# Second products two sequences behind the first, two sets of transposed rows, layer norm moved to the head of VectorE's list

## The reference

```python
h = gelu(einsum('bsh,bhi->bsi', x, Wi[expert]) + bi[expert])     # 512 -> 2048
o = einsum('bsi,bih->bsh', h, Wo[expert]) + bo[expert]           # 2048 -> 512
r = o + x
y = (r - mean(r)) * rsqrt(var(r) + 1e-12) * gamma[expert] + beta[expert]
x0, x1, x2, x3 = features of y by fours
out = stack([x0*ct + x1*st, -x0*st + x1*ct, x2*cp + x3*sp, -x2*sp + x3*cp])
```

## Time and profile before

| | |
|---|---|
| time of 3 runs, median (lowest to highest) | 2797.54 us (2796.03 to 2798.73) |
| profiled execution, its own time | 2791.9 us |
| its span, first to last instruction | 2790.2 us |
| TensorE, matmuls busy | 2679.8 us, 96% |
| VectorE busy | 1959.2 us, 70% |
| GpSimd busy | 1368.4 us, 49% |
| ScalarE busy | 930.0 us, 33% |
| granted TensorE clock, mean | 0.991 of full speed |

### The profile page before, as it was taken

How to read it: one execution, slowest core, us unless ns; L and a number is a source line. 1 busy time by engine, 2 the same in 40 slices (tenths; PEclk the granted TensorE clock), 3 DMA queues, 4 the chain that set the end, 5 groups by cost and what they waited for, 6 DMA issues and landing times.

```text
span 2790.2 us, 54938 instructions
## 1 busy us (share of the span) xinstructions
PE 2679.8 (96%) x12306; PEld 1208.7 (43%) x12307; DVE 1959.2 (70%) x4919; ACT 930.0 (33%) x1689; POOL 1368.4 (49%) x1619
## 2 busy tenths in 40 slices
PE   2899999999999999999999999999999999999998
PEld 1344444444444444444444444444444444444443
DVE  4577677677777777777777777777766776777676
ACT  4333333333333333333333333333333333333332
POOL 4778717872017872577600577607872677500000
PEclk9899999999999999999999999999999999999999
DMA  4577556865446865658644658646776667444343
GB/s 159 143 135 191 128 134 152 182 150 118 85 94 158 179 147 129 147 126 193 151 84 93 148 126 194 149 83 166 169 150 120 166 126 175 113 92 89 83 98 65
DMA packets 742569, 376.01 MB, mean 135 GB/s; under 512 B 682816, under 2 KB 682944, under 8 KB 733824
## 3 DMA queue, kind: packets, MB, share of 16 engines
q1 hardware_dynamic: 677568, 173.95, 36.6%
q0 software_dynamic: 25984, 130.29, 14.7%
q10 hardware_dynamic: 38976, 71.32, 8.1%
HBM read 174.13 MB, written 33.55 MB: 74 GB/s over the span
## 4 chain that ended last, share of the span: by engine, by line
PE 79%; DMA 6%; DVE 5%; issue 4%; POOL 2%; DVEq 2%; ACT 1%; ACTq 0%; SPq 0%; POOLq 0%
PE o_ps L850 40%; PE z_ps L834 39%; DMA hT<-h 2%; DMA xT<-x 2%; DMA xbuf<-in_x 2%; DVE z_ps L647 1%; DVEq L196 1%; ACT z_ps L472 1%; DVE h L657 0%; ACT x L467 0%; DVE ln L674 0%; DVE y L702 0%; DVE r_ps L673 0%; ACTq L196 0%; POOL wo L340 0%
## 5 line engine op out<-in xcount | busy, mean ns | idle before, releaser
L850 PE MATMUL o_ps<-wo,hT 128*128 x6144 | 1419.7, 381 | 24.0 <-DMA hT<-h 15.7
L834 PE MATMUL z_ps<-wi,xT 128*128 x6096 | 1401.7, 380 | 31.0 <-DMA xT<-x 18.8
L850 PEld LDWEIGHTS o_ps<-wo,hT 128*128 128x128 f16 x6144 | 603.6, 98 | 758.2 <-issue 41.7
L834 PEld LDWEIGHTS z_ps<-wi,xT 128*128 128x128 f16 x6096 | 597.0, 98 | 759.6 <-issue 56.8
L472 ACT ACTIVATE z_ps<-z_ps 128x512 f32<-128x512 f32 x512 | 299.1, 584 | 1760.6 <-DVE z_ps L647 1746.2
L647 DVE SCALAR_TENSOR_TENSOR z_ps<-z_ps,tok,bi_all 128x512 f32<-128x512 f32 x512 | 387.4, 757 | 217.4 <-PE z_ps L834 156.8
L406 POOL TENSOR_TENSOR wi<-staged 128x512 f32<-128x512 f32 x112 | 117.7, 1051 | 646.6 <-DVE r_ps L667 635.5
L657 DVE SCALAR_TENSOR_TENSOR h<-z_ps,tok,h 128x512 f16<-128x512 f32 x512 | 380.2, 743 | 7.4 <-ACT h L478 6.9
L478 ACT ACTIVATE h<-z_ps,tok 128x512 f16<-128x512 f32 x512 | 351.8, 687 | 19.0
L652 DVE SCALAR_TENSOR_TENSOR x<-xbuf,tok,x 128x512 f16<-128x512 f16 (+1 forms) x128 | 121.1, 946 | 189.2 <-ACT x L467 189.2
L702 DVE SCALAR_TENSOR_TENSOR y<-r_ps,rot,y 128x128 f32<-128x128 f32 x512 | 195.2, 456 | 5.0 <-ACT y L485 2.0
(11 more groups left out here) (126 smaller groups left out, 1408.8 us busy)
## 6 DMA issues: line engine op xcount, KB each, us to landing
staged<-in_L_cond_Wi POOLq DMA_DIRECT2D x56, 1024.0 KB, 6.0
staged<-in_L_cond_Wo POOLq DMA_DIRECT2D x56, 1024.0 KB, 6.8
xbuf<-in_x ACTq DMA_DIRECT2D x128, 256.0 KB, 3.6
out<-y ACTq DMA_DIRECT2D x128, 256.0 KB, 3.5
hT<-h SPq DMA_TRANSPOSE x512, 4.2
bi_all<-in_L_cond_bi POOLq DMA_DIRECT2D x7, 1024.0 KB, 9.7
wi<-in_L_cond_Wi SPq DMA_DIRECT2D x4, 1024.0 KB, 8.7
wo<-in_L_cond_Wo ACTq DMA_DIRECT2D x4, 1024.0 KB, 11.4
```

The lines of the kernel that those rows point to most:

```text
L834: last = t.matmul(z_ps[:, n, :], xT16[:, j, a, k, :], wi16[:, bass.ds(b, 1), w, k, cs], start=(k == 0 and (a, w) == PASSES[0]), stop=(k == ...
L850: last = t.matmul(o_ps[:, j, :], hT16[:, n, a, c, :], wo16[:, bass.ds(b, 1), w, n * GC + c, :], start=(n == 0 and c == 0 and (a, w) == PAS ...
```

## The change

- TensorE's second products run for sequence s - 2 in pass s, where they ran for s - 1. `hT16` gets two sets, and the numbers of the program's start lie in the second of them. The written-out passes at both ends of the loop are others, and there is one pass more.
- VectorE's residual, layer norm and rotation are those of sequence s - 3. All of the layer norm (moments, root, normalise) stands in one piece behind the residual and the two lo halves, ahead of the scale of h and of all four banks. The table loads for the buffer and the rank stand behind it.
- ScalarE takes the hi half of the next x first in its pass; the turn is that of sequence s - 3 and the store that of s - 4. The wait for the transposed x stands ahead of the last GELU of the pass before.
- GpSimd may overwrite a Wi once the first products of its sequences are done (`s_z`), where it waited for their residual (`s_res`). `xbuf` has six slots.

```diff
@@ pipeline
-            iteration(1, 1)
-            iteration(2, 0)
+            for s in range(1, 5):
+                iteration(s, s % 2)
             with engine.Fori(0, (S - 8) // 4) as i:
                 for j in range(4):
-                    iteration(i * 4 + (3 + j), (1 + j) % 2, True)
-            for s in range(3 + (S - 8) // 4 * 4, S + 2):
+                    iteration(i * 4 + (5 + j), (1 + j) % 2, True)
+            for s in range(5 + (S - 8) // 4 * 4, S + 3):
                 iteration(s, s % 2)
@@ gpsimd
-                            pool.wait_ge(s_res, before)
+                            pool.wait_ge(s_z, before * NB)
@@ scalar, iteration
+                ahead, here, last = there(s, 1, inner), there(s, 0, inner), there(s, -3, inner)
                 if ahead:
-                    act.wait_ge(s_xT, (s + 1) * 16)
+                    if isinstance(s, int):
+                        act.wait_ge(s_xT, (s + 1) * 16)
+                    hi_x(s + 1)
                 if here:
                     gelu_bank(s, k, 0)
-                if ahead:
-                    hi_x(s + 1)
-                if there(s, -3, inner):
-                    store(s - 3)
+                if there(s, -4, inner):
+                    store(s - 4)
                 if here:
                     gelu_bank(s, k, 1)
                 if there(s, 2, inner):
                     fetch_x(s + 2, k)
-                if there(s, -3, inner):
-                    act.wait_ge(s_y, (s - 2) * 16)
+                if there(s, -4, inner):
+                    act.wait_ge(s_y, (s - 3) * 16)
                 if here:
                     gelu_bank(s, k, 2)
                 if last:
-                    turn_own(s - 2)
+                    turn_own(s - 3)
+                if there(s, 2, inner):
+                    act.wait_ge(s_xT, (s + 2) * 16)
                 if here:
                     gelu_bank(s, k, 3)
                 if there(s, 2, inner):
                     sum_x(s + 2, k)
@@ vector, iteration
                 if last:
-                    b2 = slot_value(dve, BUF, s - 2, 1)
-                    residual(s - 2, k, b2)
-                if here:
-                    dve.wait_ge(s_wi, r + 1)
-                    scale_h(s, k, b)
-                    z_bank(s, 0, b)
+                    b3 = slot_value(dve, BUF, s - 3, 1)
+                    residual(s - 3, 1 - k, b3)
                 if back:
                     lo_group(s - 1, 1 - k, NB - 1)
                 if ahead:
                     lo_x(s + 1)
                 if last:
-                    moments(s - 2, b2)
+                    moments(s - 3, b3)
+                    root()
+                    normalise(s - 3, b3)
                 if here:
+                    b, r = (0, 0) if not inner and s == 0 else (slot_value(dve, BUF, s, 1), slot_value(dve, RANK, s, E - 1))
+                    dve.wait_ge(s_wi, r + 1)
+                    scale_h(s, k, b)
+                    z_bank(s, 0, b)
                     z_bank(s, 1, b)
                     lo_group(s, k, 0)
-                if last:
-                    root()
-                    normalise(s - 2, b2)
-                if here:
                     z_bank(s, 2, b)
@@ tensor, iteration
                     if back:
-                        second_product(s - 1, 1 - k, n, b1)
+                        second_product(s - 2, k, n, b2)
```

More of the change, by code:

```diff
@@ L75, in expert_mlp_rotate_kernel @@
     QN = H * I // P // Q
-    XB = 5
+    XB = 6
     WO_SPLIT = 2
@@ L261, in iteration @@
                 if there(s, -1, inner):
-                    transpose_h(NB - 1)
+                    transpose_h(NB - 1, 1 - k)
                 if there(s, 1, inner):
@@ L266, in iteration @@
                     for n in range(NB - 1):
-                        transpose_h(n)
+                        transpose_h(n, k)
             iteration(-1, 1)
@@ L494, in iteration @@
             def iteration(s, k, inner=False):
-                ahead, here, last = there(s, 1, inner), there(s, 0, inner), there(s, -2, inner)
+                ahead, here, last = there(s, 1, inner), there(s, 0, inner), there(s, -3, inner)
                 if ahead:
-                    act.wait_ge(s_xT, (s + 1) * 16)
+                    if isinstance(s, int):
+                        act.wait_ge(s_xT, (s + 1) * 16)
+                    hi_x(s + 1)
                 if here:
                     gelu_bank(s, k, 0)
-                if ahead:
-                    hi_x(s + 1)
-                if there(s, -3, inner):
-                    store(s - 3)
+                if there(s, -4, inner):
+                    store(s - 4)
                 if here:
@@ L709, in iteration @@
                 ahead, here = there(s, 1, inner), there(s, 0, inner)
-                back, last = there(s, -1, inner), there(s, -2, inner)
-                b = r = b2 = None
-                if here and not inner and s == 0:
-                    b, r = 0, 0
-                elif here:
-                    b, r = slot_value(dve, BUF, s, 1), slot_value(dve, RANK, s, E - 1)
+                back, last = there(s, -1, inner), there(s, -3, inner)
                 if ahead:
@@ L742, in iteration @@
                 if last:
[L743 removed]
+                    rotate(s - 3)
             raws = [w[:, 1].rearrange("p a k n -> p (a k n)").bitcast(F32) for w in (wi16, wo16)]
@@ L849, in second_product @@
                     for a, w in PASSES:
-                        last = t.matmul(o_ps[:, j, :], hT16[:, n, a, c, :], wo16[:, bass.ds(b, 1), w, n * GC + c, :],
+                        last = t.matmul(o_ps[:, j, :], hT16[:, j, n, a, c, :], wo16[:, bass.ds(b, 1), w, n * GC + c, :],
                                         start=(n == 0 and c == 0 and (a, w) == PASSES[0]),
@@ L856, in iteration @@
             def iteration(s, k, inner=False):
-                back, here = there(s, -1, inner), there(s, 0, inner)
-                boot = not inner and s == 1
-                b = b1 = r1 = None
+                back, here = there(s, -2, inner), there(s, 0, inner)
+                boot = not inner and s == 2
+                b = b2 = r2 = None
                 if back:
-                    b1 = slot_value(pe, BUF, s - 1, 1)
+                    b2 = slot_value(pe, BUF, s - 2, 1)
                     if not boot:
-                        r1 = slot_value(pe, RANK, s - 1, E - 1)
+                        r2 = slot_value(pe, RANK, s - 2, E - 1)
                 if here:
@@ L873, in iteration @@
                     elif back and n == 0:
-                        pe.wait_ge(s_wo, r1 + 1)
-                        if inner or s >= 3:
-                            pe.wait_ge(s_res, s - 2)
+                        pe.wait_ge(s_wo, r2 + 1)
+                        if inner or s >= 4:
+                            pe.wait_ge(s_res, s - 3)
                     if back:
-                        second_product(s - 1, 1 - k, n, b1)
+                        second_product(s - 2, k, n, b2)
             pe.wait_ge(s_onehot, 2)
```

11 lines of the change are left out of this document (5 added, 6 removed).

## The result

The changed kernel takes 3033.89 us (median of 4 runs, 3023.11 to 3059.04) against 2797.22 us of the kernel before beside it: a ratio of 1.0885, 95% interval 1.0848 to 1.0922. It is slower, as forecast, but by twice the 4.2% that I forecast, and the median lies 4 us above the end of my range.

What follows compares the result with a forecast made beforehand. TensorE bounds the kernel before, at 20.8 us a pass; in the changed kernel a ring of 21.2 us would. Start 115 + passes 2629 + late transfers 110 + drain 54 = 2908 us of span, so 2915 us, 4.2% slower; range 2805 to 3030.

Steps and rivals of the forecast that it cites:

- 124 x 21.2: Passes between 115 us and VectorE's pass 127, all taken as 21.2 us long: 2629 us.
- The ring: VectorE's scale of x, layer norm, ScalarE's GELUs, store, landing and back: 21.2 us a pass, above TensorE's 20.8.
- The table loads: VectorE, last normalise to scale of h: taken as 1.9 us, bounds 0.7 and 2.7.
- the landing: Store's landing, taken as 2.0 us, an edge of the ring that holds back ScalarE's GELU of bank 2.
- my own sign of being wrong: Store landed before the GELU of bank 2 is ready, needing that GELU wait-free within 2 us of the store.
- rival 2: Store's landing keeps its 3.5 us, so the ring is 22.7 us and the total time 3100 us; chance 0.11.
- Late transfers: Loads of x and stores that meet weight fetches lose their cover: 110 us, bounds 0 and 190.
- Start: VectorE's pass with the first layer norm starts at 115 us, not 130.62, a gain of 16 us.
- hT: TensorE's 15.7 us of waits for transposed rows should go, each transpose getting 20.7 us more.
- Drain: End of the kernel after pass 127 starts: 54 us against about 43, so 11 us lost.
- Rivals 1, 3 and 4: 1: table loads cost 0.7, ring 20.0, 2805 us, chance 0.14; 3: 2755 us, chance 0.11; 4: no change, 2797, 0.04.
- Rival 3: TensorE stays the bound, late transfers vanish in the two-deep backlog: 2755 us; chance 0.11.

Runs made afterwards that it cites:

- h3: Changed kernel with VectorE's list in its old order and 16 empty instructions at the head of VectorE's program: 2759.11 us, ratio 0.9895.
- h1: Changed kernel with 16 empty instructions at the head of VectorE's program, nothing else: 2920.40 us, ratio 1.0472.
- h7: Changed kernel with the store ahead of ScalarE's first GELU and 16 empty instructions at the head of VectorE's program: 2807.43 us, ratio 1.0076.
- g4: Changed kernel with eight passes written out ahead of the loop instead of four, so the loop starts from pass 9: 2917.36 us, ratio 1.0452.
- f4: Changed kernel without 96 of the 112 weight fetches, GpSimd's arithmetic kept: 2944.59 us, ratio 1.0551.
- e2: Changed kernel with ScalarE's store issued ahead of the GELU of bank 0: 2923.65 us, ratio 1.0444.
- g3: Changed kernel, layer norm still at the head, with a loop of two, table loads at the head, store and x load before the first GELU: 2771.91 us, ratio 0.9933.
- h5: Changed kernel with VectorE's old order, store and x load before the first GELU, loop of four, 16 empty VectorE instructions: 2750.48 us, ratio 0.9861.
- e1: Changed kernel with VectorE's list in its old order, everything else as changed: 2788.59 us, ratio 0.9997.
- f3: Changed kernel with VectorE's old order and a loop of two passes instead of four: 2764.40 us, ratio 0.9911.
- e3: Kernel before with the layer norm at the head of VectorE's list and ScalarE's hi half of x first: 2927.99 us, ratio 1.0468.
- g2: Changed kernel with VectorE's old order, a loop of two, and store and x load ahead of the first GELU: 2761.86 us, ratio 0.9893.

## Why the prediction was right in kind and short in size

By ratios of the runs, in us of 2797 and taken one after the other (the loading costs the changed kernel 116, but 103 with the store first and 29 in the old order): the rest of the change gives 29 back (h3); the layer norm's place costs 161 (h1 less h3), of which 111 hang on the store (h1 less h7); loading VectorE's code again on every trip costs 116 (changed kernel less h1). That is +248, the 8.85% measured.

By the steps of the forecast, for the median run:

- **The failed step: "124 x 21.2", one length for all passes.** The jump of the loop is a term that I put at nothing. I had read the jump of the loop in TensorE's rows alone, as 0.17 us, and asked only what is issued, not what code has to be there. A quiet trip takes 88.5 us and without the loading 85.3 (g4): 3.2 us in each of some 31 trips, 98 us. The line of queue 14 can't be had from the kernel before; but VectorE's loop begins 102 instructions later in the changed list and is 3 longer, which could be read ahead of a run, though not yet what it costs.
- **The ring.** Without the loading a pass is 21.3 us (85.3 / 4), forecast 21.2: 15 us over the run. Every term up to bias 0 is within 0.25 us. The table loads cost 1.79 (last normalise to scale of h; taken 1.9, bounds 0.7 and 2.7). One edge of it failed too: the landing doesn't hold up the GELU of bank 2 in a quiet pass, as I had it, and my own sign of being wrong, a store that has landed before the GELU of bank 2 is ready, holds in about 100 of 128 passes. The edge is ScalarE's own list between the store and that GELU, 2.62 us (2917.67 to 2920.29) where I put 2.0 for the landing. That the ring still comes out 0.1 us from the forecast is partly luck: in g4's quiet trip the GELU of bank 2 is on the mean 0.3 us late (+17.4) and what follows it 0.2 us shorter than I had it (3.9). The landing itself is 2.0 as taken, so rival 2 is wrong though its time is the nearer one, and so is, for this queue, the 2.6 us by the formula of the Trainium skill (DMA: Bandwidth & Descriptors, section "Anatomy of one DMA — SWDGE (gpsimd) path") for the other kind of queue.
- **Late transfers, 110 us:** 3033.9 less 1.7 (time over the span), 115.1 (start), 123 quiet passes of 22.1 (2721) and 68.5 (from the last scale of x, at 2988.8, to the end) leaves 128. The size was near, the make-up wasn't: I gave 93 to x loads in 31 passes and 17 to stores; the profile charges x loads 44.1 us in 17, and late stores hold up the GELU of bank 2 in 26 passes, by 60 us. The 128 aren't all transfers, as f4 gives back 93.
- **Start:** the third scale with a layer norm behind it stands at 115.1, forecast 115. **hT:** its wait is gone. **Drain:** 68.5 us from the last scale of x, forecast 21.2 + 54; pass 127 has no next x and is shorter, and the last three stores are 9.36 and 10.34 us apart (forecast 10.3).
- **Rivals 1, 3 and 4** needed a ring under TensorE's 20.8; e2, h7 and g3 show what it would have taken. Rival 3's mechanism, TensorE the bound and late transfers lost in the backlog, is real: h3 and h5 are that kernel, at 2759 and 2750 us, and 2755 was its forecast.

Open: how many packets VectorE holds. Bodies in three stay, bodies in four are loaded again with five packets a trip, which fits a store of four with one loaded ahead; no run tells that apart.

## What to carry to other kernels

When operations move to the head of an engine's list, follow the loop that they close through the other engines' lists, DMA issues and landings included, and compare it with the bound engine's pass; here one store behind one GELU decided two thirds of the cost of the layer norm's place. When the profile charges a wait to a DMA, compare its landing with the start of what waited: most of the 122 waits for the store were the engine's own list. Operations moved for cover keep it only where something still runs: in a ring, the places that were idle before are not. And in a hardware loop, look at queue 14 of the page for each version: if its packets grow with the trips, move or shorten the body before judging the change itself.

## What the runs showed of the hardware

- A hardware loop whose VectorE body of 331 instructions begins at the wrong place is loaded anew on every trip: 145 more packets of 8 KB in 30 trips, 2.6 to 4.1 us of idle VectorE at the jumps shown, and 1.0% (e1 against h3) to 4.1% (changed kernel against h1) of the run, more where the pass has less slack. Sixteen empty instructions ahead of it cure that; 56 of them made the kernel before 2.6% slower.
- A DMA issue on ScalarE takes 0.36 us and leaves it idle for 0.60 us ahead of the next activation (changed kernel, 2918.13).
- A store of 256 KB that ScalarE issues 0.8 us behind a transpose lands in 3.4 to 3.8 us by the median (before, e1, h3, f3); issued 3 us or more behind the last one, in 2.0 to 2.4 (changed kernel, e2, e3, g2, g3, h5, h7). In the changed kernel a transpose issued 0.7 us behind the store doesn't slow it: 2.0.
